# VectorE's order in the first routed stage and in the last stage, and swapped waits, in an eight-sublayer model on one core

## What is computed

```
h = tok(x)
h = h + L0_attn(layer_norm(h))     # recurrence h = tanh(h A' + x_t) over 36 steps, then a norm
h = h + L0_ffn(layer_norm(h))      # first routed stage: 8 experts, top 1
h = h + L1_attn(layer_norm(h))     # state-space scan
h = h + L1_ffn(layer_norm(h))      # 4 dense experts, top 2 weights
h = h + L2_attn(layer_norm(h))     # gated recurrence
h = h + L2_ffn(layer_norm(h))      # second routed stage: 8 experts, top 2, and a shared one
h = h + L3_attn(layer_norm(h))     # linear recurrence
h = h + L3_ffn(layer_norm(h))      # third routed stage: 7 experts, top 2, and a shared one
# routed stage:  y = sum over chosen experts of weight * expert(x)   (+ shared(x))
```

## Time and profile before

| | |
|---|---|
| median of 3 runs | 765.29 us (763.47 to 765.63) |
| the profiled execution, its own time | 762.75 us |
| its span in the profile | 760.9 us |
| mean granted TensorE clock | 0.987 of full |
| busy: TensorE, VectorE, ScalarE, GpSimd | 679.5, 344.8, 257.3, 133.2 us |
| DMA, mean over the span | 189 GB/s |

### The profile page before, as it was taken

How to read it: one execution, slowest core, us unless ns; L and a number is a source line. 1 busy time by engine, 2 the same in 40 slices (tenths; PEclk the granted TensorE clock), 3 DMA queues, 4 the chain that set the end, 5 groups by cost and what they waited for, 6 DMA issues and landing times.

```text
span 760.9 us, 15979 instructions
## 1 busy us (share of the span) xinstructions
PE 679.5 (89%) x6469; PEld 520.0 (68%) x6469; DVE 344.8 (45%) x1009; ACT 257.3 (34%) x638; POOL 133.2 (18%) x100
## 2 busy tenths in 40 slices
PE   9888869898865698989988999999986999999996
PEld 6666658785533356765754678888964557889885
DVE  3328640004899875558669641111136762111113
ACT  0433334553633405573592322222210112222221
POOL 2000100002199900123050130000040040000004
PEclk9999989999999999999999999999998999999998
DMA  8960079925456230000000879998327147899903
GB/s 309 407 232 1 17 232 413 382 102 209 146 128 151 78 125 0 1 2 0 1 0 18 349 250 381 378 363 350 138 61 319 48 189 233 337 368 367 359 25 93
DMA packets 30931, 143.83 MB, mean 189 GB/s; under 512 B 4624, under 2 KB 16720, under 8 KB 24336
## 3 DMA queue, kind: packets, MB, share of 16 engines
q1 hardware_dynamic: 23888, 132.86, 47.3%
q0 software_dynamic: 2240, 5.90, 2.4%
q10 hardware_dynamic: 4736, 4.13, 1.7%
HBM read 133.15 MB, written 9.71 MB: 188 GB/s over the span
## 4 chain that ended last, share of the span: by engine, by line
PE 61%; DVE 13%; issue 10%; DMA 6%; POOL 5%; ACT 4%; SPq 0%; DVEq 0%; POOLq 0%; ACTq 0%
PE PS L555 57%; DVE arena L2047 5%; DMA y_slots<-arena 2%; POOL arena L1522 2%; PE PS L614 2%; DMA x_slots<-XH,posu 1%; PE PS L578 1%; DMA arena<-bc_scratch 1%; POOL arena L1548 1%; DVE arena L2172 1%; DMA arena<-y_slots,posu 1%; POOL arena L1535 1%; DMA arena<-w_tok 1%; DVE stats L1584 1%; POOL arena L1551 1%
## 5 line engine op out<-in xcount | busy, mean ns | idle before, releaser
L555 PE MATMUL PS<-arena 128*64 128x64 f32 (+4 forms) x3060 | 244.2, 265 | 11.8 <-issue 3.3
L555 PEld LDWEIGHTS PS<-arena 128*64 128x64 f32 (+1 forms) x3060 | 207.6, 155 | 39.7 <-issue 15.4
L1831 DVE TENSOR_TENSOR arena<-arena,PS 128x384 f32<-128x384 f32 (+1 forms) x66 | 26.8, 407 | 179.6 <-ACT arena L1204 179.6
L555 PE MATMUL PS<-warm 128*128 128x512 bf16 (+2 forms) x401 | 91.2, 361 | 9.9 <-DVE mv L1591 8.6
L1522 POOL DMA_INDIRECT arena<-y_slots,posu x25 | 23.6, 946 | 310.0 <-DMA y_slots<-arena 303.3
L1204 ACT ACTIVATE arena<-PS 128x384 f32<-128x384 f32 (+1 forms) x66 | 27.3, 414 | 135.7 <-PE PS L555 135.7
L555 PEld LDWEIGHTS PS<-warm 128*128 128x128 bf16 (+1 forms) x401 | 36.7, 101 | 47.2 <-DVE mv L1591 9.6
L1535 POOL TENSOR_TENSOR arena<-arena 128x1152 f32<-128x1152 f32 x16 | 56.3, 3520 | 33.0 <-DVE arena L2047 32.9
L555 PE MATMUL PS<-arena,ident 128*128 128x512 f32 (+1 forms) x128 | 38.0, 440 | 21.7 <-POOL arena L1535 21.7
L555 PE MATMUL PS<-arena,wsh 128*64 128x64 f32 (+3 forms) x680 | 50.5, 249 | 3.8 <-ACT arena L1196 3.2
L1509 POOL DMA_INDIRECT x_slots<-XH,posu x25 | 24.2, 968 | 157.9 <-DVE posu L1770 151.2
(11 more groups left out here) (296 smaller groups left out, 924.6 us busy)
## 6 DMA issues: line engine op xcount, KB each, us to landing
arena<-w_moe SPq DMA_DIRECT2D x24, 2176.0 KB, 9.3
arena<-w_moe SPq DMA_DIRECT2D x9, 2052.0 KB, 12.1
wsh<-w_moe SPq DMA_DIRECT2D x8, 2176.0 KB, 9.4
arena<-bc_scratch SPq DMA_DIRECT2D x32, 288.0 KB, 3.8
wsh<-w_moe SPq DMA_DIRECT2D x3, 2052.0 KB, 11.1
y_slots<-arena ACTq DMA_DIRECT2D x19, 128.0 KB, 9.0
wx<-w_moe SPq DMA_DIRECT2D x1, 2176.0 KB, 17.6
wx<-w_sh SPq DMA_DIRECT2D x1, 2176.0 KB, 8.4
```

The lines of the kernel that those rows point to most:

```text
L555: return nc.tensor.matmul(out_, l, r, start=start, stop=stop, skip_group_check=True)
L1831: ins = v.tensor_tensor(firsts(hid_b[x][:, 0:full], n_), firsts(sg_s[x][:, 0:full], n_), firsts(PS[:, 2 * x + 1, 0:full], n_), ALU.mult)
```

## The change

1. `newton` waits first for `root_ready` and then joins (it was the other way round), and `collect_tile` joins behind the wait for a row and ahead of its operation, not behind the operation.
2. In the first routed stage `collect` takes the gathered rows of tiles between the joined sums: rows of tiles 0 and 1, pair 0, statistics 0 and 1, pair 1, rows 2 and 3, statistics 2 and 3, pair 2, row 4, statistics 4. In the second stage the joined sums stay behind tile 0's rows, and the statistics of a tile come behind the rows of the next.
3. At the end of the third stage all six shared products come ahead of gathered rows. Then the rows of tiles 0 to 2, the shared sums of tiles 3 and 4, and last the gathered rows of tiles 3 and 4, which now release these tiles' stores. Tiles 0 to 2 are released behind the shared sums.
4. The one-time semaphores of set-up are counted on one semaphore for GpSimd (`pool_set`) and one for VectorE (`dve_set`). On ScalarE the wait for `root_set` inside `xt_by_step` goes, and a wait for `dve_set` stands ahead of the wait for the constants.

The hunks that only rename a wait (on TensorE, and ScalarE's for `h_zero` and `comb_pad`) are left out.

```diff
--- before.py
+++ after.py
@@ -437,7 +437,7 @@
             load(wlruD_s[:, :, :], w_lru[:, 4:6], "lru")
 
 
-            sp.wait_ge(sem("pool_const"), 2)
+            sp.wait_ge(sem("pool_set"), 4)
             for at in range(0, XROWS, SB):
                 sp.dma_start(x_slots[at:at + SB, :], zrow[:, :]).then_inc(sem("slots_zero"), 16)
             for at in UNSENT:
@@ -1141,7 +1141,6 @@
 
             def xt_by_step():
 
-                act.wait_ge(sem("root_set"), 1)
                 inverse_root()
                 for q, pieces in ((0, ((0, 7, 0, L), (7, 1, 0, 4))), (2, ((14, 1, 8, L - 8), (15, 1, 0, L)))):
                     act.wait_ge(sem("xt_psum"), q + 1)
@@ -1270,6 +1269,7 @@
                             .then_inc(sem("yt_ready"), 1)
 
 
+            act.wait_ge(sem("dve_set"), 1)
             act.wait_ge(sem("ld_const"), 16 * 6)
             nc.scalar.activation(lru_c[:, 0:1], col("nu"), ACT.Exp).then_inc(sem("lru_a"), 1)
             nc.scalar.activation(lru_c[:, 2:3], col("theta"), ACT.Exp).then_inc(sem("lru_a"), 1)
@@ -1476,12 +1476,12 @@
 
         @block.gpsimd
         def _(pool):
-            nc.gpsimd.memset(warm[:, :], 0.0).then_inc(sem("warm_ready"), 1)
-            nc.gpsimd.iota(iota8[:, :], pattern=[[1, E]], base=0, channel_multiplier=0).then_inc(sem("iota"), 1)
-            nc.gpsimd.memset(ones_b[:, :], 1.0).then_inc(sem("pool_const"), 1)
+            nc.gpsimd.memset(warm[:, :], 0.0).then_inc(sem("pool_set"), 1)
+            nc.gpsimd.iota(iota8[:, :], pattern=[[1, E]], base=0, channel_multiplier=0).then_inc(sem("pool_set"), 1)
+            nc.gpsimd.memset(ones_b[:, :], 1.0).then_inc(sem("pool_set"), 1)
             nc.gpsimd.memset(bias_p[:, :], 0.0).then_inc(sem("bias_split"), 1)
-            nc.gpsimd.memset(zrow[:, :], 0.0).then_inc(sem("pool_const"), 1)
-            nc.gpsimd.memset(combT[:, :], 0.0).then_inc(sem("comb_pad"), 1)
+            nc.gpsimd.memset(zrow[:, :], 0.0).then_inc(sem("pool_set"), 1)
+            nc.gpsimd.memset(combT[:, :], 0.0).then_inc(sem("pool_set"), 1)
 
 
             pool.wait_ge(sem("ld_const"), 16 * 6)
@@ -1599,8 +1599,8 @@
 
             def newton(kind=0):
 
-                join()
                 dve.wait_ge(sem("root_ready"), roots[0])
+                join()
                 flat = lambda x: x[:, :, :].rearrange("p j n -> p (j n)")
                 return v.tensor_tensor_scan(flat(root[kind]), flat(root_mul[kind]), flat(root_add[kind]), 0.0, ALU.mult, ALU.add)
 
@@ -1814,8 +1814,6 @@
             def shared(name, steps, halves=(0, 1), first=0):
 
                 for c in range(steps * halves[0] + first, steps * (halves[-1] + 1)):
-                    if halves == (1,) and c > steps + 1:
-                        collect_tile(name, c - steps - 2, 2, (3, 2))
                     shared_product(name, steps, c)
 
             def routed(name):
@@ -1841,33 +1839,57 @@
 
                 for k in range(choices):
                     dve.wait_ge(sem(f"row{k}{j}"), 16 * uses[k])
-                    link(v.scalar_tensor_tensor(tile(H, j), Yg[0:TILE_N[j], k, j * D:(j + 1) * D], wgt[0:TILE_N[j], k, j:j + 1],
+                    join()
+                    mark(v.scalar_tensor_tensor(tile(H, j), Yg[0:TILE_N[j], k, j * D:(j + 1) * D], wgt[0:TILE_N[j], k, j:j + 1],
                                                 tile(H, j), ALU.mult, ALU.add))
 
             def collect(name, choices, uses):
 
-                for j in range(NT):
-                    collect_tile(name, j, choices, uses)
-                    if j == 0:
-                        for q, (j0, n) in enumerate(PAIRS):
-                            if name == "ffn0":
-                                tile_in(2 * NT, j0)
-                            else:
-                                dve.wait_ge(sem("joined"), min(j0 + 2, NT))
-                            ins = v.tensor_tensor(pair(H, q), pair(H, q),
-                                                  PS[0:TILE_N[j0], (4, 6, 7)[q], 0:n * D].rearrange("p (j d) -> p j d", d=D),
-                                                  ALU.add)
-                            if name == "ffn0" and n == 1:
-                                ins.then_inc(sem("side_added"), 1)
-                                dve.wait_ge(sem("side_added"), 1)
-                            else:
-                                mark(ins)
-                        join()
+                def joined_pair(q):
+
+                    j0, n = PAIRS[q]
+                    if name == "ffn0":
+                        tile_in(2 * NT, j0)
+                    else:
+                        dve.wait_ge(sem("joined"), min(j0 + 2, NT))
+                    join()
+                    ins = v.tensor_tensor(pair(H, q), pair(H, q),
+                                          PS[0:TILE_N[j0], (4, 6, 7)[q], 0:n * D].rearrange("p (j d) -> p j d", d=D), ALU.add)
+                    if name == "ffn0" and n == 1:
+                        ins.then_inc(sem("side_added"), 1)
+                        dve.wait_ge(sem("side_added"), 1)
+                    else:
+                        mark(ins)
+
+                def whole(j):
+                    join()
                     tile_stats(tile(H, j), j)
+
+                if name == "ffn0":
+                    collect_tile(name, 0, choices, uses)
+                    collect_tile(name, 1, choices, uses)
+                    joined_pair(0)
+                    whole(0)
+                    whole(1)
+                    joined_pair(1)
+                    collect_tile(name, 2, choices, uses)
+                    collect_tile(name, 3, choices, uses)
+                    whole(2)
+                    whole(3)
+                    joined_pair(2)
+                    collect_tile(name, 4, choices, uses)
+                else:
+                    collect_tile(name, 0, choices, uses)
+                    for q in range(len(PAIRS)):
+                        joined_pair(q)
+                    for j in range(1, NT):
+                        collect_tile(name, j, choices, uses)
+                        whole(j - 1)
+                whole(NT - 1)
                 variances()
 
 
-            dve.wait_ge(sem("iota"), 1)
+            dve.wait_ge(sem("pool_set"), 2)
             mark(v.tensor_copy(iota8f[:, :], iota8[:, :]))
             mark(v.memset(mv[:, :, :], 1.0))
             mark(v.memset(root_eps[:, 0:1], LN_EPS))
@@ -1881,8 +1903,7 @@
             mark(v.memset(XT[:, :, T:NT * TT], 0.0))
             mark(v.memset(h_z[:, :, :, :], 0.0))
             join()
-            dve.sem_inc(sem("xt_pad"), 1)
-            dve.sem_inc(sem("root_set"), 1)
+            dve.sem_inc(sem("dve_set"), 1)
 
             dve.wait_ge(sem("ld_tokb"), 16)
             for q, (j0, n) in enumerate(PAIRS):
@@ -2243,12 +2264,22 @@
             side_tiles(8 * NT, 3, range(0, 3))
             routed("ffn3")
             shared("ffn3", CH2, (1,))
-            for j in range(CH2 - 2, NT):
+            early = 3
+            for j in range(early):
                 collect_tile("ffn3", j, 2, (3, 2))
-            dve.sem_inc(sem("out_tile"), 3)
             for j in range(3, NT):
                 dve.wait_ge(sem("tm_ready"), 9 * NT)
-                v.tensor_tensor(tile(H, j), tile(H, j), TM(j), ALU.add).then_inc(sem("out_tile"), 1)
+                mark(v.tensor_tensor(tile(H, j), tile(H, j), TM(j), ALU.add))
+            join()
+            dve.sem_inc(sem("out_tile"), early)
+            for j in range(early, NT):
+                dve.wait_ge(sem(f"row0{j}"), 48)
+                mark(v.scalar_tensor_tensor(tile(H, j), Yg[0:TILE_N[j], 0, j * D:(j + 1) * D], wgt[0:TILE_N[j], 0, j:j + 1],
+                                            tile(H, j), ALU.mult, ALU.add))
+                dve.wait_ge(sem(f"row1{j}"), 32)
+                join()
+                v.scalar_tensor_tensor(tile(H, j), Yg[0:TILE_N[j], 1, j * D:(j + 1) * D], wgt[0:TILE_N[j], 1, j:j + 1],
+                                       tile(H, j), ALU.mult, ALU.add).then_inc(sem("out_tile"), 1)
 
 
 def kernel(**inputs):
```

18 lines of the change are left out of this document (9 added, 9 removed).

## The result

| | before | changed |
|---|---|---|
| median, us | 765.46 (762.12 to 768.05, 12 runs) | 760.88 (757.57 to 765.45, 12 runs) |
| profiled execution, its own time | 762.75 | 759.8 |
| its span | 760.9 | 757.8 |
| mean granted TensorE clock | 0.987 | 0.985 |

The ratio is 0.9938 with a 95% interval of 0.9913 to 0.9964. The forecast was 761.7 us and faster; 761.7 over 765.29 is a ratio of 0.9953. The two profiled executions differ by 3.1 us in their spans and by 3.05 us where VectorE ends (758.43 and 755.38).

What follows compares the result with a forecast made beforehand. It took the kernel as one long relay of waits with no engine the bound everywhere; its terms summed to -3.58 us, which from the median of 765.29 gave 761.7 us, range 759.0 to 764.0.

Steps and rivals of the forecast that it cites:

- Start: ScalarE's start: second table load no longer waits for the variances, first root 1.26 us sooner, and -0.05 for the scan's wait.
- rival (b): First norm: ScalarE's two loads bound it, by late constants or idle time behind each; 763.0 or 764.3 us; chance 0.10.
- The case of that rival in which each load holds the engine as long again: ScalarE's start: 1.28 us more behind each load, root at 22.9, +1.3 us; total 764.3 us; chance within the shared 0.10.
- Newton swaps: Swapped waits ahead of newton scans: six places gain 0.05 us each, -0.30; the norm inside attn1 loses 0.05.
- the sign rule: Newton scans: a swap gains 0.05 us where the root ends last, costs 0.05 where VectorE's own step does.
- First routed stage: VectorE's collection: rows and statistics hidden under TensorE's last sums, aggregation at 182.87 instead of 183.83, -0.96 us.
- Rival (c): First routed stage: the new order does nothing, something else ends last there; total 762.7 us; chance 0.05.
- Second routed stage: End of its collection: two statistics instead of one follow the last row, the rest paced by gathers; +0.37 us.
- Tail: Third stage's end: six products in a row, VectorE then works serially, last sum ends sooner, stores cost the same; -1.38 us.
- Rival (a): Tail gives nothing: TensorE paces the last chunks, four rows added behind, +2.0 instead of -1.38; total 765.1 us; chance 0.07.
- Renames: Renamed set-up semaphores: the waits on them are fulfilled long before, so 0 us.
- Rival (d): Recurrence: TensorE's clock falls to 1.2 GHz for a quarter of the stretch, +8 us; total 769.7 us; chance 0.03.

Runs made afterwards that it cites:

- stage1_only: The kernel before with only the first routed stage's collection in the new order, rows' waits and joins placed as before: 763.78 us, ratio 0.9973.
- after_start_undone: The changed kernel with ScalarE's wait for `dve_set` put back ahead of the first root: 763.14 us, ratio 0.9976 to the kernel before.

## Why the prediction was right

The sum was -3.58 us; the profiled pair gave -3.1 by its spans, the two comparisons of medians -4.6 (765.46 to 760.88) and -5.3 (766.14 to 760.8). Point by point:

1. **Start, -1.31**: in the pair aggregation to scan went from 2.22 to 0.81, so -1.41, of which 0.07 is the scan's wait. Right, by the mechanism given, and with some luck: the constants landed at 16.82, not at 17.14. The part of rival (b) that spoke of late constants is half true. In four of the eight profiles with the new start the load ends last, by 0.1 to 0.6 us, and the mean of the six kernels with the swap too is 1.00, so -1.2. The case of that rival in which each load holds the engine as long again is excluded: the root stands 0.01 us behind its load. The Trainium skill ("ScalarE: Activation LUTs", What ACT_TABLE_LOAD costs) adds a drain to each load; in these traces none followed the two loads.
2. **Newton swaps, -0.30 and +0.05**: the size is 0.06 to 0.08, not 0.05, and the sign rule holds. Three places were counted wrongly: ahead of ffn0 0.07 is gained where 0 was counted, ahead of ffn3 nothing where 0.05 was, and the norm behind the recurrence, which wasn't counted, loses 0.06. The seven places that can be read come to -0.21.
3. **First routed stage, -0.96**: -0.94 in the pair; the four other profiles of this form took 10.67 to 10.70 us, so -0.9. Rival (c) falls. The statistics' joins cost as taken: a pair takes 0.89 with the join, 0.75 without, 0.14 where 0.11 was taken. The Trainium skill ("VectorE: DVE Perf Modes", The DRAIN you can't avoid) reports eight copies as long with a semaphore behind each as with one behind the last; a pair of statistics here differs by those 0.14 us.
4. **Second routed stage, +0.37 (0.30 to 0.45)**: **this term was too small.** The four profiles with the new order took 15.28 to 15.51 us (mean 15.41), the ten with the old order 14.78 to 14.87: +0.6. The extra statistic and its join are as counted, about 0.4. What the step "all but the end is covered by gathers, which pace it" left out is that the gathers themselves don't keep their pace: the seventh takes 1.04, 1.09, 1.15 and 1.16 us in those four, and 0.94 to 1.01 in the other ten. What goes with it can be read from the traces. In the four an addition of a gathered row on VectorE, both of whose large inputs lie in SBUF, began 0.14 to 0.26 us ahead of this gather and ended 0.22, 0.27, 0.33 and 0.34 us behind its start, and the gather is longer by just that less 0.12. The same holds for each of the eleven indirect DMAs, of 700 in the fourteen profiles, that took over 0.02 us longer than elsewhere. Statistics and sums out of PSUM that ran across a gather's start cost it 0.01 us at most. No kernel was built to test it.
5. **Tail, -1.38**: -1.37 in the profiled pair to the end of the last store's issue, and 1.0 to 1.4 by the six old tails without idle products (16.83 to 17.26, mean 17.0, against 15.8), so **-1.2** as a mean. Rival (a), that the tail gives nothing, falls. The size is nearly right, the way to it only in part. "TensorE has full clock until then" was misread: it fell at 754.57, and TensorE's 3.68 us from the last product to the first sum are one of the prices that the old tail can have (2.6 where the clock stood). And "stores cost the same 2.47 behind it" holds where the clock had fallen, and not where it stood: there VectorE ends up to 1 us earlier (15.5), but the last store's issue, held up by the queue of stores that starts only behind tile 4's rows, doesn't. So at VectorE's end the order gives 0.3 us where the clock stood and 1.3 where it had fallen, and at the last store 1.0 to 1.2 and 1.4. That it gives nearly the same in both is luck as far as the forecast goes: the earlier release of the first three stores, which it took to be worth nothing, is what gives it where the clock stood. In the new tail the first three are issued by the time that VectorE ends, and VectorE is the bound.
6. **Renames, 0**: nothing that can be read moved with them.

Rival (d), the clock in the recurrence, didn't occur: the granted clock was 1.00 from the first to the second aggregation in all fourteen profiles. That stretch took 44.2 to 44.8 us in all eight profiles with the new start and 45.5 to 46.7 in the six without, 1.6 less on average, so some 0.3 more than the scan's start moved. What gives it isn't known.

With the mean sizes: -1.2 - 0.21 - 0.9 - 0.06 (its scan) + 0.6 - 1.2 is -3.0 us. The medians say 4.6 and 5.3 with 2 us of uncertainty or more. What the rest is, if it is anything, these runs don't settle: 3.0 lies inside the first interval (0.9964 to 0.9913 is 2.8 to 6.7 us) and below the second (4.4 to 9.2). Both show the changed kernel faster; how near 3.58 came to what the change is worth, they don't show. The parts alone, with 0.999 for the start's two timings together, 0.998, 0.9973 and 0.9987, add up to -0.7% or 5.4 us, each uncertain by 0.2% or more, and without the second stage's loss.

## What to carry to other kernels

Of two waits on one instruction, write first the one that ends last: the later-written one is a sequencer instruction of its own and costs about 0.07 us, at whichever place it is the last to be fulfilled; better still, put an operation on another tile between two dependent ones, which took rows from 0.59 to 0.42 us apart. A function table load goes behind the wait that stands ahead of it, so keep the wait for data that comes late as the only one on the instruction that needs the load. And before a kernel's end is priced from one profile, follow it to the last store, not to the last engine, and see whether TensorE's durations in it are those of the full clock: by VectorE's end this order was worth 0.3 us in one execution and 1.3 in the next, by the last store 1.0 to 1.4. Release early what can be stored early.

## What the runs showed that had not been expected

- Stretches that no kernel touches move more than any term of the sum. From the first stage's reload of scattered rows to its first gather the fourteen profiles took 65.08 to 69.30 us. Beside that a part worth 1.4 us is hard to see in ten runs.
- TensorE's clock fell among the dense experts, at holes of at most 0.8 us, in five of the fourteen profiles (13.6 us for the stretch instead of 11.9). All five have the new order of the first stage, which ends over 100 us ahead; three with the new order didn't show it. Whether that is chance is open.
- Behind the second stage's idle time the windows of before show the clock at 1.00 again from 582 us on (TensorE's first idle product starts at 576.26), those of stage1_only only from 588 on (578.87), and there aggregation to aggregation took 26.30 us. In after_start_undone it was 26.10, in the other twelve profiles 23.95 to 24.39. In these two the clock stood at 0.50 for 13.7 us, in the others for 3.4 to 10.2.
- A gather on GpSimd got up to 0.2 us slower with nothing changed on GpSimd, when an addition of a gathered row on VectorE, begun at least 0.13 us before, ran more than 0.14 us into it.
- In the old tail five stores in a queue ended last, in five of the seven profiles, and hid most of what TensorE's clock did ahead of them.
